# A graph layer with routed experts: short routing records instead of whole rows in the expert queues

## The chip, the cores and the metric

One core of one Trainium2 chip. The metric is device time in microseconds (us), the median of three runs: 3566.1 us before (3565.01 to 3568.53).

## What is computed

`x` is 50,000 rows of 256 values, with 25,000 weighted edges sorted by destination.

```python
x = x + segment_sum(layernorm(x).f16[dst] * weight.f16, src)      # first layer
h = layernorm(x)
logits = h @ gate_w + gate_b; idx = argmax(probs); prb = probs[idx]
pos = rank of the token among those with the same idx, in order    # capacity C = 7813 of 8 experts
buf[idx, pos] = h where pos < C
ybuf = relu(buf @ w1 + b1) @ w2 + b2                               # 256 -> 1024 -> 256 for each expert
x = x + nan_to_num(ybuf[idx, pos] * prb * (pos < C))
```

## The kernel before, in words

Five engines run their own programs and meet at semaphores. There are three stages with a barrier between them.

**Edges** (`edge_and_constants`): normalises gathered rows and adds the messages into `agg` in HBM. The change does not touch it.

**Routing** (`route_tokens`): 49 steps of 1,024 tokens, eight groups of 128. In step s, VectorE adds x and agg (L661) into one of four `pay` rows, takes statistics (L667, L676), writes token number, mean and reciprocal deviation, and between them works on earlier steps: `slot` of s-2 (L733 to L748) turns ranks into rows of the expert queues, and `choice` of s-1 (L700 to L723) takes the best expert from the logits. ScalarE takes the square root (L553), normalises in four quarters of two groups (L570) and copies what PE has turned out of PSUM (L566). PE turns each quarter (four blocks, L619), multiplies it by the gate weights (eight matmuls, L604), and ranks the tokens of the step before (L588, L590). SyncE loads x and agg two steps ahead and stores x + agg into `out`. GpSimd (POOL) issues eight scatters a step (L539), which write whole `pay` rows, 256 values and 11 of record, into `slots`, a queue for each expert.

**Experts** (`run_experts`): 92 units, 82 whole (512 tokens) and 10 half, over eight experts. SyncE loads a unit's rows from `slots` into one of four `u_pay` buffers (L941), as soon as the unit four earlier is finished. VectorE normalises unit u+1 (L1073, L1078), splits the hidden values of u (L1098, eight blocks), then, after the second layer, scales and cleans y (L1110 to L1129) and adds the token's row (L1131). PE runs the first layer (L1170, eight blocks of six matmuls), turns unit u+1 (L1153), and runs the second layer (L1181). ScalarE makes relu (L1046) and its rounded part (L1050) for each block, and xhi (L1028). A first layer's block f waits for the relu of block f-2, as `u_H` has two halves. POOL scatters the result into `out` (L1010, one issue per 128 tokens), waits until it has landed and frees `yo` and the token buffer; VectorE waits for that ahead of L1123. At the first unit of an expert POOL also splits the next expert's weights (L985, L987) before any scatter.

The orders on each engine are written out by hand, so an instruction never passes one that stands before it.

Of the kernel before, what the change touches and what calls it, by code (L numbers as in the profile page):

```python
# [21 lines left out]
ALU = mybir.AluOpType  # L22
ACT = mybir.ActivationFunctionType
# [15 lines left out]
MEAN, RSTD, TOKEN, LOGIT = 256, 257, 258, 259  # L39
RING = 4  # L40
# [341 lines left out]
def route_tokens(nc, ctx, t):  # L382
# [7 lines left out]
    C, QUEUE = t["C"], t["QUEUE"]  # L390
# [3 lines left out]
    assert LAST % RING == 0  # L394

    def base_of(i, r):
        s = RING * i + r
        return N - STEP if (isinstance(i, int) and s == LAST) else i * (RING * STEP) + r * STEP

# [6 lines left out]
    xt = sb("xt", [P, 2, G, D], F32)  # L406
    at = sb("at", [P, 2, G, D], F16)
    pay = sb("pay", [P, RING, G, W], F32)
# [3 lines left out]
    gb = sb("gb", [P, E], F32)  # L412
    stats = sb("t_stats", [P, G, 6], F32)
    mv = sb("t_mv", [P, 2, G, 2], F32)
# [3 lines left out]
    token = sb("token", [P, G], F32)  # L418
# [3 lines left out]
    limit = sb("limit", [P, E], F32)  # L422
    fresh = sb("fresh", [P, G], F16)
    lg = sb("lg", [P, G, E], F32)
    cand = sb("cand", [P, G, E], F32)
    top = sb("top", [P, G], F32)
    best = sb("best", [P, G], F32)
    hot = sb("hot", [P, 2, G, E], F16)
    place = sb("place", [P, 2, G + 1, E], F32)
    kept_hot = sb("kept_hot", [P, G, E], F32)  # L430
    own = sb("own", [P, G, E], F32)
    kept = sb("kept", [P, G], F32)
    where = sb("where", [P, G], F32)
    slot_i = sb("slot_i", [P, RING, G], I32)
    ones, before, ident, eps = t["ones"], t["before"], t["ident"], t["eps"]

    ps_T = ctx.enter_context(nc.psum_tensor("ps_T", [P, G * KD, P], F32))
# [5 lines left out]
    bound_i = sb("bound_i", [1, E, t["UMAX"]], I32)  # L443
    filled = sb("filled", [1, E], F32)
    queued = sb("queued", [1, E], F32)
    over = sb("over", [1, E, t["UMAX"]], F32)
    count = sb("count", [1, E], F32)
    begin = sb("begin", [1, E + 1], F32)
    offset = sb("offset", [1, E], F32)
    beyond = sb("beyond", [1, E, t["UMAX"]], F32)  # L450
    wholes = sb("wholes", [1, E], F32)
    halves = sb("halves", [1, E], F32)
# [7 lines left out]
    loaded = [sem(f"t_loaded{r}") for r in range(2)]  # L460
# [3 lines left out]
    norm_ready = sem("norm_ready")  # L464
    h_ready = sem("h_ready")
# [9 lines left out]
    step_b = sem("t_step_b")  # L475

    BANKS = G * KD * P // 512
    PER_BANK = G * KD // BANKS

    with nc.Block() as block:  # L480

        @block.sync
        def _(sp):
# [3 lines left out]
            def load(i, r):  # L487
                s = RING * i + r

                if not (isinstance(i, int) and s < 2):  # L490
                    sp.wait_ge(x1_ready, s - 1)
                b = base_of(i, r)
                sp.dma_start(xt[:, r % 2], x[bass.ds(b, STEP), :].rearrange("(g p) d -> p g d", p=P))\
# [10 lines left out]
            for r in range(1, RING):  # L504
                load(0, r)
                store(0, r - 1, base_of(0, r - 1))
# [735 lines left out]
```

## Time and profile before

| | before |
|---|---|
| median of the runs | 3566.1 us |
| the profiled execution, and its span | 3569.06 us, 3567.3 us |
| PE busy | 2846.6 us (80%) |
| PE weight loads | 2603.9 us (73%) |
| VectorE busy | 2245.0 us (63%) |
| ScalarE busy | 1539.7 us (43%) |
| GpSimd busy | 1724.4 us (48%) |
| moved by DMA | 374.74 MB |

Engines are named PE (matmul), PEld (weight load), DVE (VectorE), ACT (ScalarE), POOL (GpSimd), SP (SyncE). L12 is line 12 of the kernel before. The page of the profile has busy times over the whole span; the three stages have different limits, so they are read apart. An idle engine costs something only where others wait for it.

### The profile page before, as it was taken

The page shows a single profiled execution, that of the slowest core. Times are in us where ns is not written, and L with a number is a line of the kernel's source. Part 1 is how long each engine was busy: PE and PEld are TensorE (multiplying, and loading weights), DVE is VectorE, ACT ScalarE, POOL GpSimd, SP SyncE. Part 2 cuts the span into 40 slices and gives each one's busy share as a digit, 9 for nine tenths or more (in the row PEclk, how much of TensorE's full clock was granted, in tenths as well). Part 3 has the DMA queues.
Part 4 walks back from the last instruction along what each step waited for, and adds up shares of the span by engine and source line. Part 5 has one row for each costly group of instructions (what it writes and reads, how often), then busy time and mean ns, then how long its engine had stood idle before and what let it go on. Part 6 is the DMA issues. An engine that isn't in the chain of part 4 may idle for free.

```text
span 3567.3 us, 60077 instructions
## 1 busy us (share of the span) xinstructions
PE 2846.6 (80%) x18806; PEld 2603.9 (73%) x18807; DVE 2245.0 (63%) x5836; ACT 1539.7 (43%) x2638; POOL 1724.4 (48%) x1183
## 2 busy tenths in 40 slices
PE   4553434067677777499999999999999999999998
PEld 3443433067676667399898999888999989998987
DVE  5645555076566566377666677676677776667666
ACT  2322222044444444255444555454455545554443
POOL 4788887635555566333434333343433343334323
PEclk8666666555555555699999999999999999999999
DMA  8544444388787776311211211121211121111111
GB/s 313 153 89 77 87 78 86 29 269 252 249 259 248 228 240 207 115 48 56 66 57 44 72 48 52 49 67 57 67 48 47 56 67 47 48 51 49 42 47 37
DMA packets 306007, 374.74 MB, mean 105 GB/s; under 512 B 34887, under 2 KB 266340, under 8 KB 302608
## 3 DMA queue, kind: packets, MB, share of 16 engines
q1 hardware_dynamic: 224608, 202.49, 19.3%
q0 software_dynamic: 77728, 145.22, 14.9%
q10 hardware_dynamic: 3600, 26.22, 1.8%
q8 instruction: 28, 0.46, 0.1%
q14 instruction: 43, 0.35, 0.0%
HBM read 185.42 MB, written 196.46 MB: 107 GB/s over the span
## 4 chain that ended last, share of the span: by engine, by line
PE 53%; DVE 4%; issue 1%; DVEq 0%; DMA 0%; SPq 0%; ACT 0%; POOL 0%; POOLq 0%; ACTq 0%
PE u_Y L1181 27%; PE u_H L1170 23%; PE u_T L1153 3%; DVE y L1110 1%; DVE yo L1129 1%; DVE yo L1126 1%; DVE y L1115 0%; DVE hn L1078 0%; DVE low L1120 0%; DVE hlo L1098 0%; DVE yo L1124 0%; DMA slots<-blank 0%; DMA u_pay<-slots 0%; DVE scales L1073 0%; DVEq L1078 0%
## 5 line engine op out<-in xcount | busy, mean ns | idle before, releaser
L1010 POOL DMA_INDIRECT out_x<-yo,u_token x348 | 668.5, 1921 | 1261.4 <-DVE yo L1131 1179.5
L1181 PE MATMUL u_Y<-whi,hhi 128*128 128x256 f32 x2784 | 784.2, 282 | 1.5 <-DVE hlo L1098 1.5
L1181 PE MATMUL u_Y<-wlo,hhi 128*128 128x256 f32 x2784 | 775.4, 279 | 0.0
L1181 PE MATMUL u_Y<-whi,hlo 128*128 128x256 f32 x2784 | 774.8, 278 | 0.0
L1046 ACT ACTIVATE hm<-u_H,b1e 128x512 f32<-128x512 f32 (+1 forms) x736 | 487.9, 663 | 639.8 <-PE u_H L1170 627.0
L539 POOL DMA_INDIRECT slots<-pay,slot_i x392 | 415.3, 1059 | 325.5 <-DVE slot_i L748 210.3
L1170 PE MATMUL u_H<-xhi,whi 128*128 128x512 f32 (+1 forms) x1472 | 563.6, 383 | 8.0 <-issue 5.5
L1170 PE MATMUL u_H<-xhi,wlo 128*128 128x512 f32 (+1 forms) x1472 | 562.2, 382 | 0.0
L1170 PE MATMUL u_H<-xlo,whi 128*128 128x512 f32 (+1 forms) x1472 | 560.2, 381 | 0.0
L1181 PEld LDWEIGHTS u_Y<-whi,hhi 128*128 128x128 f32 x2784 | 528.4, 190 | 1.7 <-DVE hlo L1098 1.7
L1181 PEld LDWEIGHTS u_Y<-wlo,hhi 128*128 128x128 f32 x2784 | 528.8, 190 | 0.0
L1181 PEld LDWEIGHTS u_Y<-whi,hlo 128*128 128x128 f32 x2784 | 528.1, 190 | 0.0
L1110 DVE TENSOR_TENSOR y<-u_Y,b2e 128x256 f32<-128x256 f32 x348 | 123.9, 418 | 555.2 <-PE u_Y L1181 555.2
L1050 ACT ACTIVATE hhi<-hm 128x512 fp32r<-128x512 f32 (+1 forms) x736 | 448.7, 610 | 23.3
L1098 DVE TENSOR_TENSOR hlo<-hm,hhi 128x512 fp32r<-128x512 f32 (+1 forms) x736 | 454.0, 692 | 2.9 <-ACT hhi L1050 2.9
L604 PEld LDWEIGHTS ps_L<-gw,hT 128*128 128x128 f32 x1568 | 350.3, 332 | 43.9 <-ACT hT L566 26.5
L604 PE MATMUL ps_L<-gw,hT 128*128 128x8 f32 x1568 | 344.0, 353 | 39.8 <-ACT hT L566 24.5
L212 POOL DMA_INDIRECT agg<-sums,target x200 | 329.5, 1648 | 83.7 <-issue 58.8
L1170 PEld LDWEIGHTS u_H<-xhi,whi 128*128 128x128 f32 x1472 | 277.0, 188 | 64.8 <-issue 9.8
L1170 PEld LDWEIGHTS u_H<-xlo,whi 128*128 128x128 f32 x1472 | 277.2, 188 | 53.8
L1170 PEld LDWEIGHTS u_H<-xhi,wlo 128*128 128x128 f32 x1472 | 277.4, 188 | 50.4
L619 PE MATMUL ps_T<-ident,h 128*128 128x128 f32 x784 | 206.9, 430 | 115.0 <-ACT h L570 111.8
(137 smaller groups left out, 3747.9 us busy)
## 6 DMA issues: line engine op xcount, KB each, us to landing
xt<-in_x SPq DMA_DIRECT2D x49, 1024.0 KB
out_x<-pay SPq DMA_DIRECT2D x49, 1024.0 KB
u_pay<-slots SPq DMA_DIRECT2D x93, 534.0 KB, 3.8
agg<-zeros ACTq DMA_DIRECT2D x25, 1024.0 KB
at<-agg SPq DMA_DIRECT2D x49, 512.0 KB
raw<-in_L_ffn_w POOLq DMA_DIRECT2D x14, 1024.0 KB
src_row<-in_src SPq DMA_DIRECT2D x25, 512.0 KB
slots<-blank SPq DMA_DIRECT2D x8, 801.0 KB, 5.1
```

Source lines behind the costliest of these rows:

```text
L212: pool.indirect_dma_start(out=agg[:, :], out_offset=bass.IndirectOffsetOnAxis(ap=target[:, r, c:c + 1], axis=0), in_=sums[:, r, c, :], in_ ...
L539: pool.indirect_dma_start(out=slots[:, :], out_offset=bass.IndirectOffsetOnAxis(ap=slot_i[:, r, g:g + 1], axis=0), in_=pay[:, r, g, :], in ...
L604: last = pe.matmul(logits[:, g, :], hT[:, g * KD + kd, :], gw[:, kd, :], start=(kd == 0), stop=(kd == KD - 1))
L619: last = pe.transpose(ps_T[:, n, :], h[:, q, g, kd * P:(kd + 1) * P], ident[:])
L1010: pool.indirect_dma_start(out=out[:, :], out_offset=bass.IndirectOffsetOnAxis(ap=token[:, s:s + 1], axis=0), in_=yo[:, s, :], in_offset=No ...
L1046: act.activation(hm[:, f, cols], ps_H[:, f % 2, cols], ACT.Relu, bias=b1e[:, f:f + 1])\
L1050: act.activation(hhi[:, f, cols], hm[:, f, cols], ACT.Copy).then_inc(hhi_ready, 1)
L1098: v.tensor_tensor(hlo[:, f, cols], hm[:, f, cols], hhi[:, f, cols].bitcast(F32), ALU.subtract)\
L1110: last = v.tensor_tensor(y[:, s, :], ps_Y[:, s, 0:D], b2e[:], ALU.add)
L1153: last = pe.transpose(ps_T[:, k, s * P:(s + 1) * P], hn[:, s, k * P:(k + 1) * P], ident[:])
L1170: last = pe.matmul(ps_H[:, f % 2, cols], w1_at(w, buf, k, f), a[:, k, cols], start=(j == 0), stop=(j == len(passes) - 1))
L1181: last = pe.matmul(ps_Y[:, s, 0:D], a[:, f, rows], w2_at(w, buf, f), start=(f == 0 and j == 0), stop=(f == KF - 1 and j == 2))
```

## The change

It changes the last two stages.

- *Records.* A queue entry in `slots` is 11 values (mean, reciprocal deviation, token number, eight logits), 44 bytes, and no longer carries the row. A step of routing writes x + agg to `out` only.
- *Routing.* A token's group is now its place in eight consecutive rows of one partition (`(p g)` for `(g p)`), so each partition loads and stores one long run; rings of eight (x1, records) and four (agg). PE adds nothing to x but brings agg to PSUM by an identity matmul (`aggregate`), and VectorE adds from there. The gate's bias comes in by a matmul. Ranks take 23 matmuls for 9. `deviation` of step s+1 stands in ScalarE's step s; `rank` stands ahead of the last gate; `slot` stands last in VectorE's step. The limit tests become one comparison. ScalarE writes and advances the token numbers. The first weight split moves from VectorE to POOL.
- *Experts.* SyncE loads the records of a unit; POOL gathers the rows from `out` by token number, three units ahead in count (`gather(u + LEAD)` ahead of the scatter of u); ScalarE copies records and rows into one of four buffers (`hold`), for unit u+1 after block 3 of u. Loads and gathers each have one buffer, which is free when `kept` says that the copy before is done. VectorE waits for `kept` before it normalises.

```diff
-MEAN, RSTD, TOKEN, LOGIT = 256, 257, 258, 259
-RING = 4
+MEAN, RSTD, TOKEN, LOGIT = 0, 1, 2, 3
+RING = 8
+AGGS = 4
...
+                if not (isinstance(i, int) and s < AGGS):
+                    sp.wait_ge(agg_up, s + 1 - AGGS)
+                    sp.nop(nofuse=True)
+                sp.dma_start(at[:, r % AGGS], agg[bass.ds(b, STEP), :].rearrange("(p g) d -> p g d", g=G))\
+                    .then_inc(agg_loaded[r % AGGS], 16)
+
+                if not (isinstance(i, int) and i == 0):
+                    sp.wait_ge(out_written[r], 16 * i)
+                    sp.nop(nofuse=True)
+                    sp.wait_ge(h_ready, BANKS * (s + 1 - RING))
+                    sp.nop(nofuse=True)
+                sp.dma_start(x1[:, r], x[bass.ds(b, STEP), :].rearrange("(p g) d -> p g d", g=G))\
+                    .then_inc(x_loaded[r], 16)
...
+            def body(i, r):
+                if not (isinstance(i, int) and RING * i + r < LEAD):
+                    store(*before_of(i, r, LEAD))
+                load(i, r)
...
+            pool.tensor_copy(whi[:, 0, :], raw[:]).then_inc(split, 1)
+            pool.wait_ge(split, 1)
+            pool.tensor_tensor(wlo[:, 0, :], raw[:], whi[:, 0, :].bitcast(F32), ALU.subtract).then_inc(split, 1)
...
+            def deviation(i, r):
+                s = RING * i + r
+                act.wait_ge(stats_ready, s + 1)
+                act.activation(std[:, r % 2, :], rec[:, r, :, RSTD], ACT.Sqrt, bias=eps[:, 0:1])\
+                    .then_inc(std_ready, 1)
...
+                act.activation(rec[:, r, :, TOKEN].bitcast(I32), token[:, q, :], ACT.Identity,
+                               bias=repeat[:, 0:1] if last_step else 0.0)
+                act.activation(token[:, 1 - q, :], token[:, q, :], ACT.Identity, bias=stride[:, 0:1])\
+                    .then_inc(token_next, 1)
...
+                normalise(0)
+                normalise(1)
+                copy(0)
+                normalise(2)
+                copy(1)
+                if not (isinstance(i, int) and s == LAST):
+                    deviation(*((i, r + 1) if r + 1 < RING else (i + 1, 0)))
+                normalise(3)
+                copy(2)
+                copy(3)
...
+                for g in range(G):
+                    last = pe.matmul(ps_A[:, g, :], ident16[:], at[:, r % AGGS, g, :], start=True, stop=True)
+                last.then_inc(agg_up, 1)
...
+                for g in range(G):
+                    last = pe.matmul(ranks[:, G, :], ones[:], hot[:, q, g, :],
                                      start=False, stop=(g == G - 1), skip_group_check=True)
                 last.then_inc(ranked, 1)
...
+                turn(i, r, 0)
+                turn(i, r, 1)
+                gate(i, r, 0)
+                turn(i, r, 2)
+                gate(i, r, 1)
+                turn(i, r, 3)
+                gate(i, r, 2)
+                if not (isinstance(i, int) and s == 0):
+                    rank(*before_of(i, r, 1))
+                gate(i, r, 3)
...
+            def add(i, r):
+                s = RING * i + r
+                v.wait_ge(agg_up, s + 1)
+                v.wait_ge(x_loaded[r], 16 * (i + 1))
+                v.tensor_tensor(x1[:, r], ps_A[:], x1[:, r], ALU.add).then_inc(x1_ready, 1)
...
+                v.tensor_reduce(top[:], logits, AX.X, ALU.max).then_inc(chosen, n.inc())
...
+                v.tensor_reduce(where[:], own[:], AX.X, ALU.add).then_inc(placed, n.inc())
+                v.wait_ge(placed, n.now())
...
+                v.tensor_scalar(full[:], where[:], float(C), FLAG, ALU.is_ge, ALU.mult)
+                v.scalar_tensor_tensor(out=where[:], in0=best[:, q, :], scalar=-float(QUEUE), in1=where[:],
+                                       op0=ALU.mult, op1=ALU.add).then_inc(placed, n.inc())
+                v.wait_ge(placed, n.now())
...
+                v.scalar_tensor_tensor(out=slot_i[:, r, :], in0=where[:], scalar=float(E * QUEUE), in1=full[:],
+                                       op0=ALU.add, op1=ALU.add).then_inc(slot_ready, 1)
...
+                add(i, r)
+                statistics(i, r)
+                scales(i, r)
                 if not (isinstance(i, int) and s == 0):
-                    choice(*steps_before(i, r, 1), Count((s - 1) * PER_B))
+                    choice(*before_of(i, r, 1))
+                if not (isinstance(i, int) and s < 2):
+                    slot(*before_of(i, r, 2))
...
-                    sp.wait_ge(y_ready, u + (1 - RING + SEED["y_ready"]))
+                    sp.wait_ge(kept, u + SEED["kept"])
...
+            def gather(u):
+                pool.wait_ge(rec_loaded, 16 * (u + 1))
+                pool.nop(nofuse=True)
+                pool.wait_ge(kept, u + SEED["kept"])
+                pool.nop(nofuse=True)
+                for s in range(SUB):
+                    pool.indirect_dma_start(
+                        out=x1[:, s, :], out_offset=None, in_=out[:, :],
+                        in_offset=bass.IndirectOffsetOnAxis(ap=rec[:, s, TOKEN:TOKEN + 1].bitcast(I32), axis=0),
+                        bounds_check=N - 1, oob_is_err=False,
+                    ).then_inc(gathered, 16)
+
+            for first in range(LEAD):
+                gather(first)
...
                 def unit(u, subs):
+                    gather(u + LEAD)
                     pool.wait_ge(y_ready, u + 1 + SEED["y_ready"])
                     pool.nop(nofuse=True)
                     for s in range(subs):
...
+            def hold(u):
+
+                act.wait_ge(gathered, 16 * SUB * (u + 1))
+                if not isinstance(u, int):
+                    act.wait_ge(y_ready, u + (1 - KEEP + SEED["y_ready"]))
+                    act.nop(nofuse=True)
+                act.activation(own[:, u % KEEP], rec[:], ACT.Copy)
+                act.activation(keep[:, u % KEEP], x1[:], ACT.Copy).then_inc(kept, 1)
...
+                        if f == KF // 2 - 1:
+                            hold(u + 1)
...
-                v.wait_ge(pay_loaded, 16 * (u + 1))
-                v.tensor_copy(scales[:], pay[:, u % RING, :, MEAN:RSTD + 1]).then_inc(scales_ready, 1)
+                v.wait_ge(kept, u + 1 + SEED["kept"])
+                if not isinstance(u, int):
+                    v.nop(nofuse=True)
+                v.tensor_copy(scales[:], own[:, u % KEEP, :, MEAN:RSTD + 1]).then_inc(scales_ready, 1)
```

## Rows read from the trace of the kernel before

**Rows 1.** By stage: window, length, busy us (instructions), clock, DMA share, GB/s.
```profile
723.00:1441.00 718.00, 530.35 (x2784) 503.60 (x2784) 439.24 (x1755) 321.83 (x637) 404.82 (x382) 0.50 0.77 240
...
1489.00:3567.00 2078.00, 2020.82 (x13504) 1845.10 (x13504) 1444.21 (x2821) 1050.06 (x1672) 781.77 (x374) 0.99 0.17 55
```

**Rows 2.** VectorE in one routing step, in order of time: start us, us, instruction.
```profile
742.84 2.29 DVE L661 TENSOR_TENSOR pay<-xt,at 128x2048 f32<-128x2048 f32 x1
745.05 0.22 DVE L733 TENSOR_TENSOR place<-ps_R,place 128x72 f32<-128x72 f32 x1
...
749.46 0.64 DVE L676 BATCH_NORM_AGGREGATE t_mv<-t_stats 128x2 f32<-128x6 f32 x8
...
751.85 0.22 DVE L700 TENSOR_TENSOR lg<-ps_L,gb 128x64 f32<-128x64 f32 x1 [0.96 <-PE ps_L L604]
...
753.13 0.23 DVE L723 TENSOR_TENSOR hot<-cand,best 128x64 f16<-128x64 f32 x1
```

**Rows 3.** PE and VectorE in a later step, in order of time.
```profile
1021.28 3.42 PE L604 MATMUL ps_L<-gw,hT 128*128 128x8 f32 x16
...
1031.78 0.23 DVE L700 TENSOR_TENSOR lg<-ps_L,gb 128x64 f32<-128x64 f32 x1 [8.99 <-remote]
```

**Rows 4.** Waits from 800 to 1400: who waited for whom, us, times, longest.
```profile
DVE lg L700 <- remote: 139.2, 19, 9.5
```

**Rows 5.** ScalarE in a routing step, in order of time.
```profile
1017.07 1.08 ACT L570 ACTIVATE h<-pay,t_shift 128x256 f32<-128x256 f32 x2
...
1022.01 0.29 ACT L553 ACTIVATE t_std<-t_mv,eps 128x8 f32<-128x8 f32 x1
```

**Rows 6.** PE in the step of rows 2, in order of time.
```profile
743.03 0.45 PE L590 MATMUL ps_R<-hot,ones 128*128 128x64 f16 x8
...
747.50 1.09 PE L619 MATMUL ps_T<-ident,h 128*128 128x128 f32 x4
748.39 3.42 PE L604 MATMUL ps_L<-gw,hT 128*128 128x8 f32 x16
```

**Rows 7.** The chain that ended last, in order of time: first layers of units.
```profile
1801.54 11.20 PE u_H L1170 x48
...
2369.08 10.99 PE u_H L1170 x48
2391.84 10.99 PE u_H L1170 x48
```

**Rows 8.** ScalarE in the unit that starts at 1801.54.
```profile
1807.17 0.69 ACT L1046 ACTIVATE hm<-u_H,b1e 128x512 f32<-128x512 f32 x1
...
1808.58 0.69 ACT L1046 ACTIVATE hm<-u_H,b1e 128x512 f32<-128x512 f32 x1
...
1814.03 1.01 ACT L1028 ACTIVATE xhi<-u_T 128x1024 fp32r<-128x1024 f32 x1
```

**Rows 9.** VectorE in the same unit.
```profile
1805.49 0.16 DVE L1123 COPY u_token<-u_pay 128x4 int32 x1
...
1810.55 1.38 DVE L1078 TENSOR_SCALAR hn<-u_pay,scales 128x256 f32 x4
1811.85 4.90 DVE L1098 TENSOR_TENSOR hlo<-hm,hhi 128x512 fp32r<-128x512 f32 x8
```

**Rows 10.** POOL at an expert's start, and in the unit of rows 8.
```profile
1747.96 9.38 POOL L987 TENSOR_TENSOR wlo<-raw,whi 128x4096 fp32r<-128x4096 f32 x1
...
1812.46 5.15 POOL L1010 DMA_INDIRECT out_x<-yo,u_token  x1 [0.30 <-issue]
1817.91 0.98 POOL L1010 DMA_INDIRECT out_x<-yo,u_token  x1 [0.30 <-issue]
```

**Rows 11.** PE: eight turnings, in the first unit and in a later one.
```profile
1484.73 1.94 PE L1153 MATMUL u_T<-ident,hn 128*128 128x128 f32 x8 [16.57 <-DVE hn L1078]
...
1812.58 1.03 PE L1153 MATMUL u_T<-ident,hn 128*128 128x128 f32 x8
```

**Rows 12.** DMA issues, from the page: line's tensors, queue, count, KB each, us to landing.
```profile
u_pay<-slots SPq DMA_DIRECT2D x93, 534.0 KB, 3.8
```

More of the change, by code:

```diff
@@ L652, in statistics @@
-            def statistics(i, r, n):
+            v.tensor_copy(token[:, 0, :], token_i[:]).then_inc(vector_set, 1)
+            SET = 2
+            def add(i, r):
+                s = RING * i + r
+                v.wait_ge(agg_up, s + 1)
+                v.wait_ge(x_loaded[r], 16 * (i + 1))
+                v.tensor_tensor(x1[:, r], ps_A[:], x1[:, r], ALU.add).then_inc(x1_ready, 1)
+            def statistics(i, r):
+                s = RING * i + r
+                v.wait_ge(x1_ready, s + 1)
+                for g in range(G):
+                    last = v.bn_stats(stats[:, g, :], x1[:, r, g, :])
+                last.then_inc(step, 1)
+                if not (isinstance(i, int) and i == 0):
+                    v.wait_ge(sent[r], 16 * G * i)
+                v.wait_ge(step, s + (1 + SET))
+                v.nop(nofuse=True)
+                for g in range(G):
+                    last = v.bn_aggr(rec[:, r, g, MEAN:RSTD + 1], stats[:, g, :])
+                last.then_inc(stats_ready, 1)
@@ L665, in statistics @@
-                v.wait_ge(x1_ready, s + 1)
-                for g in range(G):
-                    last = v.bn_stats(stats[:, g, :], pay[:, r, g, 0:D])
-                last.then_inc(step, n.inc())
-                if last_step:
-                    v.tensor_scalar(token[:], token[:], -float(REPEATED), None, ALU.add).then_inc(step, n.inc())
-                else:
-                    v.engine_nop().then_inc(step, n.inc())
-                v.wait_ge(step, n.now())
-                v.nop(nofuse=True)
@@ L688, in scales @@
[L688 to L694 removed]
+                n = Count(s * 4)
+                last_step = isinstance(i, int) and s == LAST
+                v.wait_ge(gated, s + 1)
+                v.tensor_reduce(top[:], logits, AX.X, ALU.max).then_inc(chosen, n.inc())
@@ L765, in _ @@
+            n = Count(S + SET)
             v.wait_ge(slot_ready, S)
[L766 removed]
+            v.tensor_scalar(queued[:], place[0:1, LAST % 2, G, :], float(C), None, ALU.min).then_inc(step, n.inc())
             v.wait_ge(step, n.now())
[L768 to L769 removed]
@@ L770, in _ @@
-            v.wait_ge(step, n.now())
-            v.tensor_tensor(over[:], queued[:].unsqueeze(2).broadcast_to([1, E, t["UMAX"]]), bound_i[:], ALU.is_gt)\
+            v.scalar_tensor_tensor(out=filled[:], in0=expert[0:1, :], scalar=float(QUEUE), in1=queued[:],
+                                   op0=ALU.mult, op1=ALU.add)
+            v.tensor_tensor(over[:], queued[:].unsqueeze(2).broadcast_to([1, E, UMAX]), bound_i[:], ALU.is_gt)\
                 .then_inc(step, n.inc())
```

401 lines of the change are left out of this document (197 added, 204 removed).

## The prediction

> **What bounds the kernel now.** I read the busy time by stage first, then one step and one unit in order of time, then the waits. The edge stage is left as it is. The routing stage takes 718 us for 49 steps, 14.65 us a step, with TensorE's granted clock at 0.50 and the DMA engines 77% busy; the expert stage takes 2078 us with PE busy for 2021 of them [rows 1]. So the expert stage is bound by PE, and whatever holds PE there shows in full. Routing is bound by a loop through four engines. An undisturbed step has its sum x + agg (L661) at 742.84 and its `hot` done at 753.36 [rows 2]: 10.5 us, far under the mean of 14.65. The difference is in steps such as the one at 1021: sixteen gate matmuls are recorded from 1021.28 to 1024.70, but VectorE, which waits only for them, goes on at 1031.78, 7.1 us late [rows 3]. I call this the late gate. Such waits sum to 139 us for L700 between 800 and 1400 [rows 4]; over the stage 29 of the 49 steps have one of the kind shown, 136 us together, 2.8 a step. Nothing in the trace names their cause; most end as a scatter into `slots` completes.
>
> **Routing, the new loop.** Removed: the bias add, the limit masks and two reductions; `pay` rows of 1068 bytes become records of 44, and x, agg and out move in long runs. Moved: the deviation (L553's work) of step s+1 now stands in ScalarE's step s, ahead of the last quarter of the normalising, and the rank stands ahead of the last gate. Take one round from "gates of s-1 done". VectorE: choice(s-1), then slot(s-2), then the sum and the statistics of s+1; none can be passed, since the order on the engine is fixed. ScalarE waits with deviation(s+1) for those statistics, and behind it in its queue stands the last quarter of step s. PE then turns that quarter, does gate 2, rank and gate 3, and only that releases choice(s). So each step holds the whole round once:
> - choice: 1.51 for six operations (751.85 to 753.36) [rows 2], five remain: 1.25
> - slot, bn_stats and bn_aggr: 5.05 from the first of slot to the end of bn_aggr (745.05 to 750.10) [rows 2]; slot loses two operations: 4.80
> - the sum: 2.29 [rows 2]
> - deviation 0.29 and 0.04 to be seen, a pair of normalisings 1.08 [rows 5]
> - turning four blocks 0.93 (recorded 1.09, but the next group starts 0.89 after it: 747.50 to 748.39); gate 2 is half of 3.42, 1.71; gate 3 again 1.71 [rows 6]
> - rank: eight matmuls take 0.45, 0.056 each [rows 6]; 23 instead of 9 make 1.30
>
> The sum is 15.4, and ten handovers of 0.04 make 15.8. Times 49 that is 774, against 718: **+56**. What I can't see is the sum read from PSUM, the many-form ranks, and the price of a handover; a bound of 1 us a step to either side gives +7 to +105. The new 8 aggregation matmuls and the bias matmul stand outside the round, where PE waits. The two new small ScalarE activations on token numbers stand ahead of the wait for `norm_ready`, which ends later: nothing, and 0.45 a step if that cover were gone.
>
> DMA can't set the step: at 77% of 14.65 the engines work 11.3 us a step [rows 1], for more bytes than the new step moves, and 11.3 is under 15.8. This holds even if a record costs as much as the row it replaces. The Trainium skill, DMA: Bandwidth & Descriptors, Specifications, says that below 512 B a DMA engine does a read-modify-write, which speaks against 44-byte records; by it the 1,024 records of a step might cost up to what the full rows did, and the sum would still be the same.
>
> The late gate: with a quarter of the stage's scatter bytes gone to almost none I expect most of it to go. The bounds are 0 and all of it, 2.8 a step or 137; I take 0.4 a step, **+20**, because the waits end with the scatters of long rows, and the first two steps, with no scatter yet, have none [rows 2]. The weight split leaves VectorE (**-2**; POOL is idle then). The end of the stage stays: the last 16 scatters are issued one by one as now.
>
> **Experts, each whole unit.** Now 22.76 us (first layers start at 2369.08 and 2391.84) [rows 7]; times with a plus are after the start of the unit at 1801.54 [rows 7]. A first layer is eight blocks of 1.37 on PE (10.99 in all). ScalarE runs relu and hhi of a block in 1.41 (1807.17 to 1808.58) [rows 8], so it is full in that time. The change puts two copies after block 3: the records (44 values; the deviation, a small operation, takes 0.29 [rows 5]) and the gathered rows (1024 values; xhi with as many takes 1.01 [rows 8]): 1.30, and some 0.05 for waits. Relu 4 ends at +7.73 (1808.58 and 0.69); PE needs it for block 6 at +8.24. So 0.5 of 1.35 is covered and 0.85 stops PE; later blocks give little back. VectorE, PE's second layer and the 7 us of ScalarE idle time behind xhi hide none of it, since they come later. I take 0.8 for 82 whole units: **+66** (0.5 to 1.1: 41 to 90). Half units wait for hn of a whole unit anyway: 0.
>
> VectorE's normalising stands first in its queue and now waits for the copies, at +8.35; its own work before ends at +8.7 and it starts hn at +9.0 (1810.55) [rows 9], so the wait is over by then. POOL now does, per unit, load wait, gather, scatter. From the copies at +8.35 the load lands 3.8 after its issue [rows 12], at +12.5; VectorE's block of hlo (4.90) [rows 9] then holds up one issue, as it makes a scatter at the same time take 5.15 instead of 0.98 [rows 10]; four gathers end near +18.5, four scatters at 1.28 near +23.7, their landing near +25. VectorE wants the buffer at +3.95 of the next unit (1805.49) [rows 9], +26.7: just covered, by under 2 us. At an expert's first unit POOL also splits weights before the gather, in two passes, the second of which takes 9.38 [rows 10], some 14 us together; there the cover is gone, the scatter lands some 5 us late, and PE stops 3 to 5. Seven times 4: **+28** (0 to 60).
>
> **Start and end.** The first unit's turning at 1484.73 [rows 11] is preceded by one load; now by load, gather (5.1 and some 2.2 to land) and copies (1.3), less some 3 for smaller blanks: +6; the first weights come later, as their load is queued behind three gathers, the third of which waits for unit 0: +4. Together **+10** (3 to 25). At the end the last scatter stands behind a gather of rows that nobody uses: **+5** (0 to 10).
>
> **Sum.** 56 + 20 - 2 + 66 + 28 + 10 + 5 = +183. The profiled execution took 3569.1 (span 3567.3, 1.8 around it), 3 above the median of 3566.1. 3569 + 183 - 3 = 3749; I say **3745**.
>
> **Rivals.**
> - *The late gate stays.* For it: the number of scatters that POOL issues in a step stays at eight, and nothing in the trace says that their bytes matter. Against: almost no bytes. It puts back 117: 3865. Chance 0.16.
> - *POOL falls behind in every unit.* The cover of 2 us is gone if gathers take longer than scatters; then each unit waits about 1 us more: 3745 + 80 = 3825. For it: one blocked issue costs 5.15 - 0.98 = 4.2 [rows 10]. Against: gathers come while VectorE has gaps. Chance 0.09.
> - *The routing stage gets the high clock*, and the change is faster. PE is asked for more in a step (14 more rank matmuls, 8 aggregations, a bias). Eight turnings take 1.94 in the first unit, just after the stage at clock 0.50, and 1.03 later at 0.99 [rows 1, 11]: PE's 5.7 us of the round would be 3.0, 2.7 less, or 132 over the stage. With expert terms at the lower ends (41, 0, 3, 0) and no late gate the sum is 56 - 132 - 2 + 44 = -34: 3532. It decides once the step falls below about 12.5 us. Against: the clock was 0.50 for all 718 us [rows 1], also in the undisturbed steps, in which PE has hardly a gap. The Trainium skill, TensorE: Matmul & The Clock Gate, Part 1, says that sustained PE activity lifts the clock from 1.2 to 2.4 GHz, and Part 4 that transposes are not counted as such. By the first the routing stage should have been fast already; the trace sides with the second. Chance 0.14.
>
> **How the numbers follow.** The forecast has 0.61. Its own range, with the bounds of the round and of the copies, is 3640 to 3820. For 8 in 10 I leave out the fast rival and the far end of the slow ones: 3585 to 3885. A measurement tells 0.2%, 7 us. Faster: 0.14 and 0.01 from the forecast's low tail; same 0.03; slower 0.82.
>
> **What the profile will show.** Right: routing steps of 15 to 17 us with ScalarE idle before the deviation (released by the statistics) and VectorE idle before choice; clock 0.50; no late gate; DMA share near 0.5. In the experts, whole units of 23.5, with PE's relu wait at block 6, and first units of an expert at 25 or more with VectorE waiting for `y_clear`. Wrong: steps below 14; a ScalarE copy that takes far less than 1 us; unit spacing still 22.76; or a wait for `y_clear` in every unit.

## The result and the profile after

| | before | after |
|---|---|---|
| median of the runs shown, us | 3565.6 (4 runs) | 3930.0 (3922.4 to 3944.6, 4 runs) |
| profiled execution (span) | 3569.1 (3567.3) | 3929.2 (3927.6) |
| first sum of routing | 723.3 | 734.1 |
| 48 steps, first sum to last | 690.3, 14.4 each | 754.6, 15.7 each |
| last sum to first unit | 75.7 | 83.9 |
| start of the first unit to the end of the last but one | 2046.1 | 2318.3 |
| whole units (82), mean | 22.94 | 26.01 |
| from there to the end | 32.0 | 36.8 |

The ratio is 1.103 (95% interval 1.100 to 1.106): 364 us slower, where the forecast's sum has 183 and its time, 3745, lies 185 below the measured 3930. Line numbers from here on are those of the changed kernel, if not said otherwise. The stages, as in [rows 1]: window, length, busy us of each engine, granted clock, DMA share, GB/s.

```profile
core 0: us, PE busy (x) PEld busy (x) DVE busy (x) ACT busy (x) POOL busy (x), PEclk, DMA share, GB/s
734.00:1489.00 755.00, 568.37 (x3801) 531.05 (x3800) 385.25 (x1424) 316.82 (x714) 352.12 (x360) 0.56 0.48 166
1572.50:3890.00 2317.50, 2117.27 (x13394) 1878.33 (x13395) 1477.68 (x2778) 1103.16 (x1837) 1142.50 (x736) 0.97 0.15 46
```

Up to the first unit the loss is 83 us, and the forecast had 84. The expert stage lost 272 where 94 were forecast: that is the whole miss. PE, which was busy for all but 57 us of the stage [rows 1], now has 200 us of gaps, and 97 more of busy time for the same matmuls.

**One routing step**, PE, ScalarE and VectorE out of three answers of the timeline (start us, us, instruction; in brackets the idle time before it and who ended it: "issue" where the profile shows nothing that the engine waited for, "remote" where it can't name who ended the wait), to be held against [rows 2, 5, 6]:

```profile
1090.98 0.31 ACT L579 ACTIVATE t_std<-rec,eps 128x8 f32<-128x8 f32 x1 [3.49 <-DVE rec L748]
1091.20 1.07 ACT L608 ACTIVATE h<-x,t_shift,rec 128x256 f32<-128x256 f32 x2
...
1092.33 1.11 PE L692 MATMUL ps_T<-ident,h 128*128 128x128 f32 x4 [3.68 <-issue]
1093.23 1.71 PE L678 MATMUL ps_L<-gw,hT 128*128 128x8 f32 x8
1094.80 0.44 PE L654 MATMUL ps_R<-hot,before 128*128 128x8 f16 x8
...
1095.52 1.22 PE L678 MATMUL ps_L<-gw,hT 128*128 128x8 f32 x5
1097.58 0.61 PE L678 MATMUL ps_L<-gw,hT 128*128 128x8 f32 x3 [0.85 <-issue]
...
1098.23 0.23 DVE L770 TENSOR_REDUCE top<-ps_L 128x8 f32<-128x64 f32 x1 [6.40 <-PE ps_L L678]
```

It is the round that the forecast drew: ScalarE waits 3.5 us with the deviation for the statistics, then the last quarter, the turn, gate 2, rank and gate 3, and only then `top`.

Gate 3 is broken in two in these rows. After five of its eight matmuls PE stands for 0.85 us, with no wait of the program between them. In the steps there are 43 such stops of over 0.3 us at the gate's matmuls, 27 us in all, and 26 of them end 1.48 to 1.61 us after the last scatter of a step is issued. The copies out of PSUM (L618) start 0.6 to 2.7 late in 15 places, 20 us together.

**One whole unit.** It starts at 1734.78 and the next at 1759.99, 25.2 us against the 22.76 of [rows 7]. Three things are new in it (`hhi` is the rounded part of the hidden values, `hlo` the rest). First, the copies behind block 3 and PE's stop at block 6:

```profile
1742.13 0.22 ACT L1129 ACTIVATE own_rec<-u_rec 128x44 f32 x1
1742.26 1.05 ACT L1130 ACTIVATE keep<-u_x 128x1024 f32 x1
1743.21 0.67 ACT L1153 ACTIVATE hm<-u_H,b1e 128x512 f32<-128x512 f32 x1
1743.93 0.50 PE L1285 MATMUL u_H<-xhi,whi 128*128 128x512 f32 x1 [0.38 <-ACT hm L1153]
```

A first layer with no other stop takes 11.59 us, against 10.99. Second, the second layer. Its matmuls start 0.120 us apart in every unit; before, as the second fence shows, 0.113 (lines 1181 are those of before):

```profile
1749.07 0.28 PE L1296 MATMUL u_Y<-whi,hlo 128*128 128x256 f32 x1
1749.19 0.28 PE L1296 MATMUL u_Y<-whi,hhi 128*128 128x256 f32 x1
1749.31 0.28 PE L1296 MATMUL u_Y<-wlo,hhi 128*128 128x256 f32 x1
```

```profile
1814.14 0.28 PE L1181 MATMUL u_Y<-whi,hhi 128*128 128x256 f32 x1
1814.26 0.28 PE L1181 MATMUL u_Y<-wlo,hhi 128*128 128x256 f32 x1
1814.37 0.28 PE L1181 MATMUL u_Y<-whi,hlo 128*128 128x256 f32 x1
```

96 of them take 11.59 us instead of 10.98, with no wait between them. Third, the end of that layer is seen late. PE goes on to this unit's first matmul at 1734.78, but VectorE's `y`, which waits only for the layer before, starts 2.2 us on. ScalarE's first relu starts at the same moment, though its block is recorded to end at 1736.3. Both are 1.2 after the last scatter's issue ends:

```profile
1734.84 0.97 POOL L1104 DMA_INDIRECT out_x<-yo,u_token  x1 [0.30 <-issue]
...
1736.98 1.42 DVE L1225 TENSOR_TENSOR y<-u_Y,b2e 128x256 f32<-128x256 f32 x4 [8.56 <-remote]
1737.05 0.69 ACT L1153 ACTIVATE hm<-u_H,b1e 128x512 f32<-128x512 f32 x1 [6.89 <-PE u_H L1285]
```

58 of the 82 whole units begin with such a late end. They take 25.2 on average (53 of them 25.0 to 25.7), those without it 23.97. Scatters tell the two kinds apart: where POOL is not through with them when the layer ends, `y` is late, and in 53 of the 58 it starts 1.0 to 1.3 us after the last issue ends (in the other five while one is under way). Where the last issue had ended 0.8 us or more before the layer did, `y` follows within 0.3 us. In the waits of VectorE in the expert stage (us, times, longest) it is the line with "remote":

```profile
DVE y L1225 <- remote: 554.6, 63, 10.1
DVE y L1225 <- PE u_Y L1296: 194.6, 27, 9.1
```

**The second unit of an expert** takes 36.5 to 37.7 us, seven times. VectorE and POOL in the one that starts at 1872.90:

```profile
1874.62 12.92 DVE L1230 TENSOR_SCALAR y<-y,prob 128x256 f32<-128x256 f32 x4
1894.27 1.38 DVE L1193 TENSOR_SCALAR hn<-keep,scales 128x256 f32 x4
...
1874.19 3.61 POOL L1063 CAST whi<-raw 128x4096 fp32r<-128x4096 f32 x1 [2.93 <-issue]
1877.89 8.97 POOL L1065 TENSOR_TENSOR wlo<-raw,whi 128x4096 fp32r<-128x4096 f32 x1
...
1895.71 1.97 PE L1268 MATMUL u_T<-ident,hn 128*128 128x128 f32 x8 [11.03 <-DVE hn L1193]
1897.69 0.41 PE L1296 MATMUL u_Y<-wlo,hhi 128*128 128x256 f32 x1
1897.90 0.41 PE L1296 MATMUL u_Y<-whi,hlo 128*128 128x256 f32 x1
```

Four small operations of 1.14 us together take 12.92 while POOL splits the weights, `hn` comes 12 us late, and PE stands for 11.0. Behind the stop PE is slower for a while: the turnings take 1.97 and not 1.03, about what they took in the first unit, behind a stage at clock 0.50 [rows 11], and the second layer 13.2. The granted clock is 0.50 from 1894 to 1898 and 1.00 from 1904 on. The same meeting of POOL and VectorE opens the routing stage:

```profile
719.36 3.59 POOL L554 CAST whi<-raw 128x4096 fp32r<-128x4096 f32 x1
719.44 3.54 DVE L722 TENSOR_SCALAR stale<-fresh 128x8 f32<-128x8 f16 x1 [0.88 <-POOL upto L550]
...
723.03 8.80 POOL L556 TENSOR_TENSOR wlo<-raw,whi 128x4096 fp32r<-128x4096 f32 x1
723.08 8.78 DVE L725 TENSOR_SCALAR prefer<-expert 128x8 f32<-128x8 f32 x1
```

Such an operation on 8 values takes 0.17 alone. The Trainium skill, SBUF — State Buffer, "SBUF: two separate sides", says that VectorE and GpSimd share a pair of ports under an exclusive lock that is held for a whole instruction; the four rows agree, with 8.78 us beside 8.80.

### The profile page after: what moved, and what is told of

It is laid out like the page before. It is cut to its first block, busy times and chain, and to the rows that moved or that the text cites. A ratio compares the mean times of both kernels' runs of the same rounds, so it can differ in the third digit from the quotient of the medians.

```text
span 3927.6 us, 63543 instructions
## 1 busy us (share of the span) xinstructions
PE 3017.3 (77%) x19982; PEld 2702.0 (69%) x19983; DVE 2257.7 (57%) x5543; ACT 1608.9 (41%) x2924; POOL 2091.7 (53%) x1568
## 4 chain that ended last, share of the span: by engine, by line
DVE 23%; PE 14%; another core or an unknown queue 13%; issue 6%; DVEq 2%; ACT 2%; POOL 0%; DMA 0%; ACTq 0%; SPq 0%; POOLq 0%
PE u_Y L1296 9%; DVE hlo L1213 7%; PE u_H L1285 4%; DVE y L1230 3%; DVE yo L1244 2%; DVE y L1225 2%; DVE yo L1241 2%; DVE xlo L1200 2%; DVE hn L1193 1%; DVE low L1235 1%; PE u_T L1268 1%; DVE yo L1239 1%; ACT hm L1153 1%; ACT keep L1130 1%
## 5 line engine op out<-in xcount | busy, mean ns | idle before, releaser
L1079 POOL DMA_INDIRECT u_x<-out_x,u_rec x380 | 693.1, 1824 | 1069.9 <-DMA u_rec<-slots 963.7
L1296 PE MATMUL u_Y<-whi,hhi 128*128 128x256 f32 x2784 | 805.4, 289 | 0.0
L1296 PE MATMUL u_Y<-wlo,hhi 128*128 128x256 f32 x2784 | 796.0, 286 | 0.0
L1296 PE MATMUL u_Y<-whi,hlo 128*128 128x256 f32 x2784 | 795.7, 286 | 0.0
L564 POOL DMA_INDIRECT slots<-rec,slot_i x392 | 383.4, 978 | 425.3 <-DVE slot_i L817 315.8
L1104 POOL DMA_INDIRECT out_x<-yo,u_token x348 | 370.6, 1065 | 110.5 <-issue 107.7
L1213 DVE TENSOR_TENSOR hlo<-hm,hhi 128x512 fp32r<-128x512 f32 (+1 forms) x736 | 429.3, 655 | 0.0
L678 PEld LDWEIGHTS ps_L<-gw,hT 128*128 128x128 f32 x1568 | 318.8, 295 | 27.3 <-issue 26.9
L678 PE MATMUL ps_L<-gw,hT 128*128 128x8 f32 x1568 | 312.0, 323 | 29.3 <-issue 28.9
L692 PE MATMUL ps_T<-ident,h 128*128 128x128 f32 x784 | 189.0, 405 | 155.6 <-issue 122.2
```

Source lines behind the costliest of these rows:

```text
L564: pool.indirect_dma_start(out=slots[:, :], out_offset=bass.IndirectOffsetOnAxis(ap=slot_i[:, r, g:g + 1], axis=0), in_=rec[:, r, g, :], in ...
L678: last = pe.matmul(logits[:, g, :], hT[:, g * KD + kd, :], gw[:, kd, :], start=False, stop=(kd == KD - 1), skip_group_check=True)
L692: last = pe.transpose(ps_T[:, k % 2, n, :], h[:, q, g, kd * P:(kd + 1) * P], ident[:])
L1079: pool.indirect_dma_start(out=x1[:, s, :], out_offset=None, in_=out[:, :], in_offset=bass.IndirectOffsetOnAxis(ap=rec[:, s, TOKEN:TOKEN + ...
L1104: pool.indirect_dma_start(out=out[:, :], out_offset=bass.IndirectOffsetOnAxis(ap=token[:, s:s + 1], axis=0), in_=yo[:, s, :], in_offset=No ...
L1213: v.tensor_tensor(hlo[:, f, cols], hm[:, f, cols], hhi[:, f, cols].bitcast(F32), ALU.subtract)\
```

## The experiments

The chips differ, in the traces above all in one thing: whether PE's work is seen late by the others around POOL's scatters ("late signals" in the expectations). The kernel before took 3566 on the chip of the record (A), 3436 to 3441 on B, 3533 on C and 3442 on D; of A and B there are traces of it. Runs are compared on one chip only. Unless said otherwise a run is on B and a single execution.

**Bases on B.**

> The kernel before, unchanged, with a profile, as a base on the same chip as the runs beside it: on the chip of the first four experiments it took 3437 where the record has 3566. Theory A: the difference is the late gate, a matter of that chip's state and not of the kernel: no step of routing ends on a gate 7 us after its last matmul, the routing takes some 130 less (590 instead of 718), and the expert stage is the same, 22.76 a whole unit. Rival B: the chips differ in all stages alike (3.6%).

> The changed kernel, unchanged, as a base on the same chip. Theory A, from the four experiments before: no late end of the second layer there, whole units of 23.97 (22.76 and 0.60 for the copies and 0.61 for the second layer), seven long ones with 12 us more: expert stage 2240, routing round 14.5, total 3800. Rival B, the late ends return: 3900.

Measured: 3440.8 and 3779.9. The kernel before has no late gate there: 48 steps take 575 us instead of 690, the DMA engines are at 0.96 in them, and the expert stage is the same but for 1.4 us (2044.7; 22.94 a whole unit).

```profile
715.00:1291.00 576.00, 502.78 (x2674) 484.29 (x2674) 427.61 (x1707) 312.09 (x616) 428.06 (x365) 0.50 0.96 296
```

The changed kernel has no late end on B: steady whole units take 24.0, the seven long ones are there, and its expert stage takes 2224.7, 180 more than before. A second execution gave 3777.2 (`b3_after`). The waits of VectorE in the expert stage of that second execution have no "remote":

```profile
DVE y L1225 <- PE u_Y L1296: 649.6, 91, 9.1
```

The change costs about the same on both chips (339 and 364), but not in the same places: on B 138 in the 48 steps and 180 in the experts, on A 64 and 272.

B shows what the changed kernel costs where nothing is late. A steady step takes 14.54 (48 steps 713.3, where A has 754.6), PE has no stop of over 0.3 us without a named wait in the steps, gate 3 takes 1.85 in each (on A 1.85 to 3.39, median 2.49), and a whole unit takes 25.1 on average where A has 26.0. So of the changed kernel's time on A 41 us in the steps and 94 in the experts are there and not on B.

**Where hhi and hlo lie.**

```diff
     token = sb("u_token", [P, SUB], I32)
+    pad = sb("pad", [P, 464], F32)      # before: 48
     hn = sb("hn", [P, SUB, D], F32)
```

> The changed kernel with one idle tile of 1856 bytes a partition ahead of hn, so that hn, xhi, xlo, hm, hhi and hlo lie at the addresses that they had in the kernel before; nothing else differs. In the changed kernel the 96 matmuls of a second layer start 0.120 us apart and the layer takes 11.59 us, in every unit, waits or not; before they stood 0.113 apart and it took 10.98. Theory A, the place of hhi and hlo against the weights in SBUF sets this pace: the layer is back at 10.98, and 82 whole units give back 0.61 each, 50 us: 3880. Rival B, the pace comes from the new program or its transfers: 11.59 stays, and the time stays at 3930.

> The kernel before with one idle tile of 192 bytes a partition ahead of hn: hn to hlo lie 192 bytes higher, so that hhi starts at 162144, which is 352 over a multiple of 1024, as whi does (34144) and as hhi did in the changed kernel (160096). No instruction differs. Theory A, the place of hhi and hlo against the weights sets the pace of the second layer: 0.120 us a matmul, 11.59 instead of 10.98 in whole units, 82 x 0.61 = 50 more than the 3437 to 3441 of the kernel before on the earlier chip: 3490. Rival B, the place does it only together with the changed program: no change.

Measured (`e1_addresses`, then `b1_before_shifted`): 3747.6, with the second layer at 10.98 in every steady unit (median unit 23.40 instead of 24.01); the gain on the base is 32, not 50, since halves and other units lose some. Theory A for the pace, though the time it gave was for A. The shifted kernel before takes 3482.1, 47 more than the 3435.5 beside it, with this pace:

```profile
2000.08 0.28 PE L1182 MATMUL u_Y<-whi,hhi 128*128 128x256 f32 x1
2000.20 0.28 PE L1182 MATMUL u_Y<-wlo,hhi 128*128 128x256 f32 x1
2000.32 0.28 PE L1182 MATMUL u_Y<-whi,hlo 128*128 128x256 f32 x1
```

Not one instruction differs from the kernel before; 192 bytes of address cost 0.61 us a second layer. The median unit loses 0.54 (23.30), since the first layer takes 10.91 there and not 10.99. In both layouts with 0.120 `hhi` and `whi` start at the same place in 1024 bytes (352), in those with 0.113 not (`hhi` at 160). That this is the rule behind it is only argued: two offsets were tried, and all tiles from `hn` to `hlo` moved together.

**The split on POOL.**

```diff
-                    split_weights(e + 1, 1 - buf)
+                    pool.wait_ge(raw_loaded, 32 * (e + 1))   # experts 2 to 7
+                    pool.sem_inc(split, 2)
```

> The changed kernel in which POOL splits the weights of experts 0 and 1 only; for the others it waits for the raw weights and counts on, and the units go on with the weights that are there (this part of the computation is left out). Theory A: in the second unit of an expert y times prob on VectorE is stopped for 12 us by the split on POOL, and PE waits behind it for hn; without the split six of the seven units of 36 to 38 us fall to 24 or 25, 6 x 12.5 = 75 us less: 3855. Rival B, the forecast's: what is late is the scatter, and with it y_clear, by some 5 us: the units give back 4 each, 24 us, so about 3905.

Measured, with the split left out: 3702.6, 77 less than the base. One long unit is left, expert 0's, whose split is still done. Theory A. The other way round, the kernel before with its scatters held back, so that the split behind them starts later:

```diff
                     pool.wait_ge(y_ready, u + 1 + SEED["y_ready"])
+                    pool.wait_ge(prob_ready, u + 2 + SEED["prob_ready"])
+                    for k in range(4):
+                        pool.memset(idle[:, k, :], 0.0).then_inc(idled, 1)
```

> The kernel before in which POOL, once yo of unit u is ready, also waits for prob of unit u + 1 (+17 of the unit) and then fills an idle tile (about 2 us) before it issues the scatters: they end some 1 us after the second layer instead of 4 ahead of it. Nothing is gathered, and no copy is added. Theory A: on a chip with late signals the second layer's end is seen 2 us late, the next relu 0.7 to 1.3, and whole units take about 1 us more; on any chip the split of the weights, now behind the late scatters, stops VectorE and PE for some 10 us in one unit of seven experts: 70 more on a chip without late signals, 150 on one with them. Rival B: the late end comes from the gathers or from the record queues, and the units stay at 22.76 apart from the split.

Measured: 3525.6, 90 more than the 3435.5 beside it; timed in three rounds on D (`b4_late_scatter`) 1.0245 (1.0228 to 1.0262). Six units take 12.5 to 13.9 more, and all steady ones the old 22.76. VectorE in one of the six, which starts at 1630.84:

```profile
1632.56 11.58 DVE L1124 TENSOR_SCALAR y<-y,prob 128x256 f32<-128x256 f32 x4
```

No gather, no copy and no short record is in this kernel. So the long units come from when the split starts: just ahead of VectorE's work on `y`. In the kernel before, the split at 1742.26 met `hlo` (8.32 for 4.90) and then a VectorE that was idle until 1754.69, and no unit was long. D has no late signals either, so this run could not show late ends.

**The copies, and where POOL's work falls.**

```diff
-                        if f == KF // 2 - 1:
-                            hold(u + 1)
                     upper(u + 1)
+                    hold(u + 2)
```

> The changed kernel with ScalarE's two copies out of the first layer: hold(u + 2) stands behind upper(u + 1), where ScalarE is idle, instead of hold(u + 1) behind block 3; gathers then come at +17 of a unit and the scatters of unit u at +10 of unit u + 1. Theory A: no stop of PE at block 6 (0.6 a unit), no late end of the second layer (1.0 on average), and the split of the weights falls into VectorE's idle time again; only the slower second layer is left, 0.61: the expert stage goes from 2318 to 2046 + 50 + 5 = 2101, total 3713. Rival B: what makes the end of the second layer late is any indirect transfer issued near it, gathers too: 1.0 to 1.5 a unit stay, 3800 to 3835.

> The changed kernel with both cures at once: the two copies behind upper(u + 1) and the idle tile that puts hhi and hlo where they were. Theory A: the terms add up, whole units are back at 22.8 to 22.9, and the expert stage takes 2055: 50 less than with the late copies alone, which took 3655, so 3605. Rival B: they overlap, because what stops PE then is VectorE's hlo or xlo: units of 23.2 or more, 3635.

Measured: 3654.9 and 3615.4. With the copies behind `upper` a first layer is back at 11.01, and the seven long units go too, while the first unit of all grows to 30.7: the first split now runs from 1540.62, and VectorE waits for PE until 1549.62. That is 125 less than the base, 49 for the copies (0.60 for 82 units) and 76 as the rest, put down to the split. With the old addresses as well the median unit is 22.78, 165 less than the base; the addresses give 39 here, and gave 32 alone. The terms add up, near enough. Late ends could not be told on this chip, which has none; `e9_all_cures`, below, has these copies on C.

> The changed kernel with POOL's two tasks in a unit in the other order: scatter of unit u, then gather of unit u + 3; ScalarE's copies stay where they are. Scatters then end some 8 us before the second layer does, gathers take their place, near +20. Theory A, the scatters make the end of the second layer late: 58 of 82 units give back 1.0 to 1.6, and whole units take 23.97, 70 to 80 us less in all: about 3855, with the seven long units still there. Rival B, any indirect transfer issued near the end of the layer does it: the time stays within 20 us of 3930.

The edit puts `gather(u + LEAD)` behind the scatters. Measured: 3754.4 and, once more, 3755.6 (`e11_scatter_first`); 22 to 26 less than the two bases, all of it in the seven long units (60 us over 24 each, in sum, instead of 86); steady units stay at 23.97. Written for chip A, both theories missed; neither could be tested here.

**Routing.**

```diff
                 number(i, r)
+                deviation(i, r)
                 act.wait_ge(norm_ready, s + 1)
...
-                if not (isinstance(i, int) and s == LAST):
-                    deviation(*((i, r + 1) if r + 1 < RING else (i + 1, 0)))
                 normalise(3)
```

> As e5_hold_addr, with one more edit in the routing: the deviation of step s stands at the head of ScalarE's step s and not ahead of the last quarter of step s - 1. Theory A, the forecast's round: the sum and the statistics of s + 1 no longer lie between choice(s - 1) and gate 2 of step s, so the step falls from 14.5 to what PE does in it, some 13 to 14 at the low clock: 48 steps, 25 to 80 less than e5_hold_addr. Rival B: PE or the loop's boundary sets the step already, and the time is that of e5_hold_addr within 10.

Measured: 3460.3, 155 less than `e5_hold_addr`: 48 steps in 564 us instead of 714. The place of one operation of 0.31 us is worth 3.1 us a step. The theory holds, its size was too small by half: freed of the round, the steps take 8.9 to 12.9, where they had been locked at 14.5.

> As e6_deviation, with the split of expert 0's weights at the start of routing done by VectorE again, as before, behind its constants. In the changed kernel POOL does it, and two VectorE operations of 0.16 us take 3.54 and 8.78 beside it, so the first sum comes at 724 instead of 715. Theory A, POOL's split stops VectorE: the first sum is back at 716 and the time is 8 less than e6_deviation (3460): 3452. Rival B, what sets the first sum is the loads of x and agg or PE's sum: no change.

The edit moves the two instructions of POOL's L554 and L556 into VectorE's program. Measured: 3428.9, 31 less: 5 at the first sum (718.9), where the theory said 8, and 27 in the steps. Why the steps gain is open; in `e6_deviation` the four steps in which the engines go back to the head of a loop (the 16th, 24th, 32nd and 40th) take 16.2 to 18.7 us, here at most 13.4.

> As e7_split_back, with the sum x + agg taken by VectorE straight from the loaded rows, as before, and PE's eight aggregation matmuls (1.87 us a step at the low clock) gone. The sum keeps its 2.29 on VectorE. Theory A, with the deviation moved a routing step is set by PE's own work (two thirds of the steps at 10 to 12.9 us for 14.2 us of PE work at the low clock, 9 or so where the clock is high): up to 1.9 less in 48 steps, 40 to 90: 3360 to 3410. Rival B, the step hangs on the round through ScalarE and VectorE, or PE, asked for less, gets the low clock more often: within 15 of e7_split_back.

Measured: 3443.0, 14 more than `e7_split_back`. Rival B, at its bound. The 48 steps take 540 and 536 us; 8 of the 14 lie between the last sum and the first unit. Without its eight aggregation matmuls PE has the granted clock of 0.50 (1.2 GHz) for the whole stage, with them part of it at 2.4 GHz; first `e7_split_back`, then this kernel, a window of 536 us in each:

```profile
719.00:1255.00 536.00, 524.74 (x3796) 490.20 (x3796) 384.47 (x1423) 321.12 (x710) 350.58 (x359) 0.61 0.69 237
```

```profile
719.00:1255.00 536.00, 528.76 (x3406) 516.95 (x3407) 383.10 (x1412) 323.52 (x710) 397.15 (x349) 0.50 0.68 237
```

**All cures together, timed.**

> The same kernel as e7_split_back, timed in five rounds against the kernel before, because a difference of 7 us in one look is about what a measurement can tell. Theory A: all four cures together (copies behind upper, hhi and hlo at their old place, the deviation at the head of its own step, the first split on VectorE) leave a routing stage that is 27 us shorter than before and an expert stage that is 20 us longer: ratio 0.998, 0.995 to 1.000. Rival B: the difference of the looks was chance, and the ratio is 1.000 to 1.005. On a chip with the late gate the kernel before would lose 125 us and this one whatever its own late ends cost.

Measured, on C: 3620.2 against 3533.2, ratio 1.0245 (1.0216 to 1.0273). On B the same kernel (`e7_split_back`, 3428.9) was 7 us under the kernel before and 9% under the changed one. On C it loses, which neither theory said for the ratio: there it is 191 us above its time on B, the kernel before 92 to 98, and 173 of the 191 are in its 48 steps (710 us instead of 536). It is not shown to beat the kernel before. POOL and VectorE in one of its routing steps on C:

```profile
1146.44 0.98 POOL L560 DMA_INDIRECT slots<-rec,slot_i  x1 [0.30 <-issue]
...
1149.14 0.22 DVE L768 TENSOR_REDUCE top<-ps_L 128x8 f32<-128x64 f32 x1 [5.97 <-remote]
```

`top` waits only for the gates, and starts 1.7 us after the eighth scatter's issue ends. Of the 32 steps from 860 to 1340 it does so in 26 within 1.46 to 1.76 us of the last scatter, however long ago the gates are recorded to have ended (0 to 7 us), and in the other six 2.0 to 2.5 after it. The step is then choice and slot, eight scatters of 1.28 and these 1.7: 14.8 instead of 11.2. PE itself stands too, as on A: 83 stops of over 0.3 us at the gate's matmuls, 63 us.

The expert stage of this run tells something on the late ends. With the copies behind `upper`, scatters have ended 1.9 us or more before a layer does, and on C the end is seen at once in 90 of 91 layers:

```profile
DVE y L1221 <- PE u_Y L1292: 548.1, 90, 8.6
```

In 75 of them a gather's issue ends between 0.4 us before the layer's end and 1.0 after it, and three more gathers may follow. So a run of gathers that has just begun does not make the end late there, which speaks for the scatters as theory A of `e3_hold_late` and `e4_scatter_first` has it; a run of gathers in full course over the end was not seen on such a chip.

> As e7_split_back, but only four of the eight record scatters of a routing step are issued (half of the records are left out; slots are filled with blank records ahead of the stage, so the expert stage computes with what is there and isn't to be read). Theory A, on a chip with late signals PE's gate is seen by VectorE only 1.7 us after the last scatter of a batch: 8 x 1.28 and 1.7 and 2.9 for choice and slot make 14.9, as e9 shows; with four scatters the batch is out of the way and the step is PE's own, 11 to 12.5 us, so routing is 110 to 170 shorter than the 710 of e9. On a chip without late signals the step is 11.2 with eight and stays so. Rival B, the lateness has nothing to do with how many are issued: 14.8 stays where it was 14.8.

Measured, on B again, with half of the records left out: 3410.7, and a step of 11.07 against 11.17. It says only that on a chip without late signals POOL's scatters don't set the step. On D, which has none either, it was 11.4 (`e12_half_scatters`, 3426).

## Why the prediction was wrong

- **Routing, the new loop (+56) and the late gate (+20).** 64 for both, of 76, and that this is so near is luck. The order of events is as forecast, and `e6_deviation` shows that the deviation's place closes the round. But the round is 14.54 us where nothing is late (B), not 15.8: the rank takes 0.72 and not 1.30, VectorE's part 8.1 and not 8.3, and the ten handovers were already in the rows. Both gates of the round go at the low clock's pace, as forecast (1.57 and 1.85 in the rows, with 3.42 in the sum; gate 3 takes 1.85 in every step on B); the gates that take 0.96 for eight matmuls stand outside it. Against that, four steps (20.7 to 21.5, at the 16th, 24th, 32nd and 40th) in which the engines go back to the head of the loop cost some 5 us each, on both chips, which I had not priced. The loop of B's length would have made 23 of the 64.
- **"Most of the late gate goes".** The other 41 are what A has over B. No gate of the steps is seen more than 1.3 us late there, but PE's stops between its matmuls and the late copies are in the same steps: the lateness took another form. And the second layer, which was never late before, now is. I had asked whether the gate's waits go with the bytes, and not where else PE could meet POOL's issues, which the change moved from +10 of a unit to its end.
- **Weight split off VectorE (-2).** Wrong in sign: the first sum comes 10.8 later. "POOL is idle then" was true and beside the point; the one engine that had to be idle was VectorE. `e7_split_back` gives 5 of it back at the first sum; where the rest comes from is open.
- **Start and end of the experts (+10, +5).** 8.2 and 4.8.
- **Copies (+66).** 0.60 a unit and not 0.8: 49 (first layers in `b0_after` and `e3_hold_late`). The step was right; the cover was 0.2 larger.
- **POOL at an expert's first unit (+28).** I named the right place, POOL late behind gather, scatter and split, and the wrong victim: not VectorE waiting for `y_clear`, but VectorE stopped in the middle of `y` times `prob` by the split. [rows 10] had the price of one engine's block for the other, 5.15 instead of 0.98, and I read it in one direction only. Seven units at 13, 93 in all (`e2_no_split`, `b2_before_late_scatter`).
- **Left at nothing: the second layer.** 50 of the miss. The sum of a unit has PE's second layer as it was. The diff adds and drops tiles ahead of `hhi`, and I took addresses for free.
- **Left at nothing: the late ends.** The same kernel's expert stage takes 94 less on B, which has none, while the stage of the kernel before is the same on both: 74 are in whole units, 19 in the nine half units, which were forecast at 0. That makes them, with the weight split, the largest part of the miss. 49, 93, 50 and 94 are 286, 14 over the 272, as not every unit pays each in full.
- **The rivals.** "The late gate stays", at 3865, was nearest in time. Part of its mechanism came true (41 us in the steps), but most of the lateness fell on other matmuls. "POOL falls behind in every unit" did not happen: the `y_clear` waits on VectorE (L1238) sum to 4 us. The high clock came for a part of the routing stage, as that rival said, and did not decide.

The steps that failed are these, then: the forecast's sum for a unit had only ScalarE's copies and `y_clear` in it (94, measured 272), and left the second layer's pace, PE's lateness and VectorE's block by the split at nothing.

What stays open is why, on A and C, other engines see PE's work only after POOL's run of scatters, and PE stands between its own matmuls in the same runs, and not on B and D. That the scatters make it so is read from the times in the traces; no edit was run on A to show it. The runs that were to separate the number and the kind of transfers were on B and D, so this wasn't tried where it shows.

## What to carry to other kernels

Work that moves on POOL has to be laid against VectorE's timeline, not against POOL's: ask which VectorE operation each long POOL instruction will meet, in both directions. A diff that adds tiles changes the address of everything allocated behind them; where PE is the bound, compare the spacing of its matmuls before any wait. And one small operation in a fixed queue, 0.31 us of deviation, can close a round through four engines and cost ten times its length.

## What the runs showed of the hardware

- A second layer of 96 matmuls takes 10.98 or 11.59 us with the same instructions, by 192 bytes of SBUF address.
- An operation of 0.17 us on VectorE took 8.78 beside a POOL operation of 8.80.
- After a stop of 11 us PE's next matmuls stand 0.21 us apart instead of 0.12, with a granted clock of 0.50, and the unit loses 2.5 us on top of the stop.
- Eight more matmuls a step (1.87 us) on PE came with a granted clock of 0.61 instead of 0.50 over the stage, and the 48 steps took 536 us instead of 540 (`e7_split_back`, `e8_sum_vector`).
- The same kernel takes 3436 to 3566 us on four chips. Between A and B 115 of the 128 us are in the 48 routing steps: on A, and in another kernel's trace on C, PE's work is seen late around POOL's scatters (58 of 82 whole units on A, 53 of them 1.0 to 1.3 us after the last scatter's issue), in the traces of B and D not.
- On A and C PE stands for 0.3 to 1.3 us between matmuls of one run with no wait between them (43 and 83 times at the gate's matmuls); on B and D such stops don't occur in the steps.
